# Scalar compares for ranks, and a lighter hand-shake in the second edge sweep of a graph kernel

## Chip, cores and metric

The kernel runs on one core of one Trainium2 chip. The metric is the device time of one execution in microseconds (us), the median of several runs.

## What is computed

Four graph layers run one after another over 6250 nodes with 128 features and 106250 edges that are sorted by receiver (`dst`). After each, the node rows are normalised: `x = layernorm(x + layer(x))`.

```python
msg = relu(concat([h[src], h[dst], w]) @ W1 + b1) @ W2 + b2     # layer 0
agg = segment_max(msg, dst); h = relu(concat([h, agg]) @ U1 + c1) @ U2 + c2
msg = relu(concat([v[src], factors[dst]]) @ Wm + bm)            # layer 1 (src: senders, dst: receivers)
agg = segment_sum(msg, src, 6250)                               # v + relu(concat([v, agg]) @ Wc + bc)
e = leaky_relu(e_l[src] + e_r[dst]); alpha = segment_softmax(e, dst)
out = segment_sum(alpha * Wh[src], dst)                         # layer 2, 4 heads of 32
h = relu(x @ W_in[0] + mean(x[src], dst) @ W_in[1])             # layer 3
h = h @ W_out[0] + mean(h[src], dst) @ W_out[1]
```

## The kernel before

The edges are cut into 208 blocks of 512 (`NB`, `EB`), each of four tiles of 128. Five sweeps go over all blocks: sweep 1 (layer 0, `edge_phase(1)`), sweep 2 (layer 1, `relation_phase`), sweep 3 (layer 2, `attention_phase`), sweeps 4 and 5 (layer 3, `edge_phase` again). A node phase follows each. Layer 1 sums over senders; its edges come in pairs that swap sender and receiver, plus loops, so this kernel walks them in receiver order too.

In every sweep a segmented scan on VectorE (DVE) runs along the edges: `scan = go * previous + value`, or a maximum. TensorE turns tiles of edges by features into features by edges ahead of the scan, and turns the scanned block back after it; ScalarE (ACT) copies it out of PSUM; it goes to memory as `scan_rows`. In sweeps 1, 3, 4 and 5 GpSimd (POOL) gathers the senders' rows with four indirect DMAs to a block (L1108, L1466). In sweep 2 the rows come ready from memory (`factor_rows`), and POOL gathers only for the following node phase (L739).

In sweeps 1, 2 and 3 the receivers' rows of a block are spread over its edges by a matrix product with a one-hot matrix `same`. DVE makes it: each of the 512 ranks of the block (type uint8, the same row on all partitions) is compared with a rank of the partition (`rank_cols`, float32), one column of `rank_cols` to each tile. It is one `tensor_tensor` of 128x512 to a block: L1261 in sweep 1, L1423 in sweep 2, L1639 in sweep 3. The scalar column is broadcast as the second tensor.

`steps(eng, n, unroll, (lag, f), ...)` writes the order of work of an engine: in step i each piece f is done for block i - lag, in the order of the list. In sweep 2:

```python
steps(sp, NB, SLOTS, (0, load), (7, store))
steps(pe, NB, SLOTS, (0, go_row), (0, senders), (2, turn_back))
steps(act, NB, SLOTS, (0, hidden), (2, keep_rows))
steps(v, NB, SLOTS, (0, same_receiver), (2, reduce))
```

SyncE (SP) issues all direct DMAs of sweep 2: four loads to a block (L1319 ranks, L1320 go marks, L1321 receiver rows, L1322 factor rows) into rings of four slots, and a store (L1328). It waits for `e_recv_free` (L1317), which ACT gives once TensorE has used a block's rows. TensorE's `go_row` (L1352) spreads the marks over 128 partitions in PSUM, `senders` (L1342, L1343) makes the layer's input, `turn_back` (L1362) turns the scanned block. Before each, it waits for data and for a buffer to be free. `chain` on ACT and DVE lets the engine wait for its own instruction before it gives its semaphores.

In sweep 3 the order on DVE is `(9, weigh), (10, add_up), (1, scores), (0, same_receiver), (1, stretch)`, on TensorE `(11, turn_back), (9, turn_weighted), (0, receiver_scores), (1, stretch)`. Every eighth step has a `stretch`: a softmax chain that goes back and forth between DVE, TensorE and ACT. The gathers go into 16 slots there, and into 8 in sweep 1.

Of the kernel before, what the change touches and what calls it, by code (L numbers as in the profile page):

```python
# [17 lines left out]
P = 128  # L18
# [5 lines left out]
EB = 512  # L24
CT = EB // P
NB = -(-E // EB)
# [59 lines left out]
def gnn_program(nc, a, out):  # L86
# [14 lines left out]
    with ctx:  # L101
# [128 lines left out]
        e_rows = sem("e_rows")  # L230
        stored = [sem(f"stored{s}") for s in range(SLOTS)]
        t_er_free = sem("t_er_free"); t_cb_free = sem("t_cb_free"); t_gath_free = sem("t_gath_free")
        e_rank = sem("e_rank"); e_rank_free = sem("e_rank_free")
        e_go = sem("e_go"); e_go_free = sem("e_go_free")
        over_cleared = sem("over_cleared"); over_made = sem("over_made")

        def part(q, s, unroll, n):
# [5 lines left out]
        with ExitStack() as pctx:  # L243
# [60 lines left out]
            with nc.Block() as block:  # L304
                @block.sync
                def _(sp):
# [78 lines left out]
                    sp.sem_inc(n_load, -32)  # L385

                    for free, n in ((n_agg_free, 2), (n_rows_free, 2), (n_x_bank_free, 1), (n_bank_free[7], 1), (n_bank_free[5], 1), (n_bank_free[3], 1),
                                    (e_gath_free, RING), (e_recv_free, SLOTS), (e_meta_free, SLOTS), (e_same_free, 2), (e_rank_free, 2), (e_go_free, 2),
                                    (e_pre_free, 2), (e_hid_free, 2), (e_msg_free, 2), (e_scan_free, 2), (e_back_free, 2),
                                    (t_er_free, 1), (t_cb_free, 1), (t_gath_free, 2 * STRETCH)):  # L390
                        sp.sem_inc(free, n)
# [694 lines left out]
        def edge_phase(k):  # L1086
# [157 lines left out]
            def vector(v):  # L1244
                if expands:
                    for s in range(2):
                        v.wait_ge(scattered[s], 16 * scatters * sum(GROUP_TILES[s::2]))
                    v.sem_inc(n_scat_all, 1)

                def chain(ins):  # L1250
                    ins.then_inc(v_done, 1)
                    v.wait_ge(v_done, 1)
                    v.sem_inc(v_done, -1)

                def same_receiver(q, s):

                    v.wait_ge(meta_in[s], 32)
                    v.sem_inc(meta_in[s], -32)
                    v.wait_ge(e_same_free, 1)
                    v.sem_inc(e_same_free, -1)  # L1260
                    v.tensor_tensor(same[s % 2][:, :, :], rank[s][:, :].rearrange("p (c e) -> p c e", e=P),  # L1261
                                    rank_cols[:, part(q, s, SLOTS, CT)].unsqueeze(2).to_broadcast([P, CT, P]), ALU.is_equal).then_inc(e_same, 1)

                def reduce(q, s):
                    if not expands:

                        v.wait_ge(meta_in[s], 16)
                        v.sem_inc(meta_in[s], -16)
                    v.wait_ge(e_msg if expands else e_pre, 1)
                    v.sem_inc(e_msg if expands else e_pre, -1)  # L1270
                    v.sem_inc(e_hid_free if expands else e_gath_free, 1)
                    v.wait_ge(e_scan_free, 1)
                    v.sem_inc(e_scan_free, -1)  # L1273
                    src = (msg_ps if expands else pre_ps)[s % 2][:, :]
                    go_on = meta[s][:, :]
                    chain(v.tensor_tensor_scan(scan[s % 2][:, :], go_on, src, scan[1 - s % 2][:, EB - 1:EB],  # L1276
                                               ALU.add if expands else ALU.mult, ALU.max if expands else ALU.add))
                    v.sem_inc(e_msg_free if expands else e_pre_free, 1)
                    v.sem_inc(e_meta_free, 1)
                    v.sem_inc(e_scan, 1)  # L1280

                if expands:
                    steps(v, NB, SLOTS, (0, same_receiver), (2, reduce))
                else:
                    steps(v, NB, SLOTS, (0, reduce))
# [3 lines left out]
        def relation_phase():  # L1289
# [42 lines left out]
            def tensor(pe):  # L1332
                def senders(q, s):

                    pe.wait_ge(e_same, 1)
                    pe.sem_inc(e_same, -1)
                    pe.wait_ge(e_pre_free, 1)
                    pe.sem_inc(e_pre_free, -1)
                    b = pre_ps[s % 2]
                    for c in range(CT):  # L1340
                        o = b[:, c * P:(c + 1) * P]
                        pe.matmul(o, factor[s][:, c, :], ident[:, :], start=True, stop=False, is_transpose=True)  # L1342
                        ins = pe.matmul(o, recv[s][:, c, :], same_ring[s][:, c, :], start=False, stop=True)  # L1343
                    ins.then_inc(e_pre, 1)

                def go_row(q, s):

                    pe.wait_ge(recv_in[s], 48)
                    pe.sem_inc(recv_in[s], -48)
                    pe.wait_ge(e_go_free, 1)  # L1350
                    pe.sem_inc(e_go_free, -1)
                    pe.matmul(go_ps[s % 2][:, :], ones_row[:, :], meta[s][0:1, :], start=True, stop=True).then_inc(e_go, 1)  # L1352

                def turn_back(q, s):

                    pe.wait_ge(e_scan, 1)
                    pe.sem_inc(e_scan, -1)

                    pe.wait_ge(e_back_free, 1)
                    pe.sem_inc(e_back_free, -1)  # L1360
                    for c in range(CT):
                        ins = pe.transpose(back_ps[s % 2][:, c * P:(c + 1) * P], scan[s % 2][:, c * P:(c + 1) * P], ident[:, :])  # L1362
                    ins.then_inc(e_back, 1)

                steps(pe, NB, SLOTS, (0, go_row), (0, senders), (2, turn_back))

            def scalar(act):
                def chain(ins):
# [4 lines left out]
                def hidden(q, s):  # L1373

                    act.wait_ge(e_pre, 1)
                    act.sem_inc(e_pre, -1)
                    act.sem_inc(e_recv_free, 1)
                    act.sem_inc(e_same_free, 1)
                    act.wait_ge(e_hid_free, 1)
                    act.sem_inc(e_hid_free, -1)  # L1380
                    chain(act.activation(hid[s % 2][:, :], pre_ps[s % 2][:, :], ACT.Relu, bias=bm[:, 0:1]))
                    act.sem_inc(e_pre_free, 1)
                    act.sem_inc(e_hid, 1)

                def keep_rows(q, s):

                    act.wait_ge(e_back, 1)
                    act.sem_inc(e_back, -1)
                    act.sem_inc(e_scan_free, 1)
                    if not (isinstance(q, int) and q == 0):  # L1390

                        act.wait_ge(stored[s], 16)
# [13 lines left out]
            def vector(v):  # L1406
                for s in range(2):
                    v.wait_ge(scattered[s], 16 * scatters * sum(GROUP_TILES[s::2]))
                v.sem_inc(n_scat_all, 1)
                v.sem_inc(e_same_free, 2)  # L1410

                def chain(ins):
                    ins.then_inc(v_done, 1)
                    v.wait_ge(v_done, 1)
                    v.sem_inc(v_done, -1)

                def same_receiver(q, s):

                    v.wait_ge(meta_in[s], 16)
                    v.sem_inc(meta_in[s], -16)  # L1420
                    v.wait_ge(e_same_free, 1)
                    v.sem_inc(e_same_free, -1)
                    v.tensor_tensor(same_ring[s][:, :, :], rank[s][:, :].rearrange("p (c e) -> p c e", e=P),  # L1423
                                    rank_cols[:, part(q, s, SLOTS, CT)].unsqueeze(2).to_broadcast([P, CT, P]), ALU.is_equal).then_inc(e_same, 1)

                def reduce(q, s):

                    v.wait_ge(e_go, 1)
                    v.sem_inc(e_go, -1)
                    v.wait_ge(e_hid, 1)  # L1430
                    v.sem_inc(e_hid, -1)
                    v.wait_ge(e_scan_free, 1)
                    v.sem_inc(e_scan_free, -1)  # L1433
                    chain(v.tensor_tensor_scan(scan[s % 2][:, :], go_ps[s % 2][:, :], hid[s % 2][:, :], scan[1 - s % 2][:, EB - 1:EB], ALU.mult, ALU.add))  # L1434
                    v.sem_inc(e_hid_free, 1)
                    v.sem_inc(e_go_free, 1)
                    v.sem_inc(e_scan, 1)

                steps(v, NB, SLOTS, (0, same_receiver), (2, reduce))

                v.wait_ge(e_same_free, 4)
                v.sem_inc(e_same_free, -2)
            return gpsimd, sync, tensor, scalar, vector

        def attention_phase():
# [176 lines left out]
            def vector(v):  # L1622
# [12 lines left out]
                def same_receiver(q, s):  # L1635

                    v.wait_ge(meta_in[s % SLOTS], 16)
                    v.sem_inc(meta_in[s % SLOTS], -16)
                    v.tensor_tensor(same[s % 2][:, :, :], rank[s % SLOTS][:, :].rearrange("p (c e) -> p c e", e=P),  # L1639
                                    rank_cols[:, part(q, s, U, CT)].unsqueeze(2).to_broadcast([P, CT, P]), ALU.is_equal).then_inc(e_same, 1)  # L1640

                def scores(q, s):

# [155 lines left out]
```

## Time and profile before

| what | us |
|---|---|
| median of 3 runs (5735.0 to 5740.53) | 5735.5 |
| the profiled execution: its own time | 5743.62 |
| the profiled execution: span of the trace | 5741.8 |
| busy in the span: TensorE / DVE / ACT / POOL | 3292.9 / 2408.0 / 1217.7 / 3673.6 |
| gathers of sweep 1, first start to last start | 357.5 to 1423.2 |
| rank compares of sweep 2, first start to last start | 1594.7 to 2167.5 |
| gathers of sweep 3, first start to last start | 2307.2 to 3382.6 |
| gathers of sweeps 4 and 5, first start to last start | 3503.2 to 5655.8 |

A span is the stretch from the first to the last instruction of the trace. "Idle before" is the time an engine stood still ahead of a group of instructions, and the name behind the arrow is what ended it; DVEq, ACTq, PEq, POOLq and SPq are the engines' own queues, where their semaphore instructions run.

### The profile page before, as it was taken

Reading aid. Unit: us, or ns where it says so; the run is one execution under the profiler, and the core shown is the slowest. Engines: PE = TensorE matmul, PEld = TensorE weight load, DVE = VectorE, ACT = ScalarE, POOL = GpSimd, SP = SyncE. Lnnn points to the kernel's source line nnn. Section 1 sums busy time; section 2 is a strip of 40 time slices with the busy share of each in tenths; the row PEclk is TensorE's granted clock in tenths of the full one; section 3 lists DMA queues with packets and bytes.
Section 4 is the critical chain, followed back from the end, with each engine's and each line's share of the span. In section 5 each row is a group of like instructions: output and inputs, shape, how many; then the busy total and the mean of one; then the engine's idle time right before and its main releaser. Section 6 shows DMA issues by size and latency. Waiting matters only on the chain. (4 is left out here: it accounts for less than half of the span.)

```text
span 5741.8 us, 88988 instructions
## 1 busy us (share of the span) xinstructions
PE 3292.9 (57%) x17957; PEld 2513.3 (44%) x17957; DVE 2408.0 (42%) x3908; ACT 1217.7 (21%) x2227; POOL 3673.6 (64%) x3810
## 2 busy tenths in 40 slices
PE   1268888888578886566666652333333443333335
PEld 0245555555356665456565652333333323333333
DVE  3323333333466665466666664222222222222224
ACT  0012222222234443122222221111111111111111
POOL 2277777777701004777777774777777767777776
PEclk7578999998799998678788875555555655555556
DMA  9969999998289996455555653444444444444443
GB/s 246 304 191 291 296 301 292 295 294 286 81 272 313 311 312 185 143 157 176 156 174 165 175 144 92 132 131 132 131 132 132 122 116 131 131 131 132 132 131 105
DMA packets 813159, 1087.16 MB, mean 189 GB/s; under 512 B 132097, under 2 KB 494202, under 8 KB 809690
## 3 DMA queue, kind: packets, MB, share of 16 engines
q1 hardware_dynamic: 371752, 390.56, 22.5%
q0 software_dynamic: 134688, 305.15, 21.1%
q10 hardware_dynamic: 306588, 390.09, 20.1%
q14 instruction: 96, 0.79, 0.0%
q8 instruction: 35, 0.57, 0.0%
HBM read 647.79 MB, written 437.96 MB: 189 GB/s over the span
## 5 line engine op out<-in xcount | busy, mean ns | idle before, releaser
L1108 POOL DMA_INDIRECT gath<-sender_table,src_cols x1664 | 1570.1, 944 | 576.3 <-issue 381.3
L1276 DVE TENSOR_TENSOR_SCAN scan<-meta,scan,bank 128x512 f32<-128x512 bf16 x624 | 798.6, 1280 | 1844.1 <-DVEq L1273 1833.9
L1163 PE MATMUL bank<-ident,gath 128*128 128x128 f32 x1664 | 464.0, 434 | 1276.1 <-DMA gath<-sender_table,src_cols 1276.1
L1466 POOL DMA_INDIRECT gath<-attention_table,src_cols x832 | 823.2, 989 | 262.9 <-issue 190.5
L1108 POOL DMA_INDIRECT gath<-joint_table,src_cols x832 | 813.3, 978 | 258.9 <-issue 188.7
L1163 PEld LDWEIGHTS bank<-ident,gath 128*128 128x128 f32 x1664 | 297.7, 217 | 1442.1 <-DMA gath<-sender_table,src_cols 1442.1
L1226 ACT ACTIVATE rows<-bank 128x512 f32<-128x512 f32 x624 | 372.6, 597 | 1995.4 <-ACTq L1224 1913.8
L1188 PE MATMUL bank<-ident,scan 128*128 128x128 f32 x2496 | 580.2, 379 | 4.8 <-PEq L1186 4.8
L1188 PEld LDWEIGHTS bank<-ident,scan 128*128 128x128 f32 x2496 | 478.9, 205 | 139.5 <-issue 139.5
L739 POOL DMA_INDIRECT gath<-scan_rows,end_i x147 | 140.9, 958 | 586.8 <-ACTq L1394 542.9
L1506 PE MATMUL bank<-recv,same 128*128 128x4 f32 x1664 | 225.5, 259 | 161.9 <-PEq L1504 161.6
L1261 DVE TENSOR_TENSOR same<-rank,rank_cols 128x512 f32<-128x512 uint8 x208 | 144.4, 694 | 412.7 <-DVEq L1260 391.1
L1506 PEld LDWEIGHTS bank<-recv,same 128*128 128x128 f32 x1664 | 218.1, 204 | 189.7 <-issue 189.7
L1170 PEld LDWEIGHTS bank<-same,recv 128*128 128x128 f32 x1664 | 224.4, 209 | 169.8 <-issue 169.8
L1211 ACT ACTIVATE hid<-bank,b 128x512 f32<-128x512 f32 x208 | 142.9, 687 | 698.9 <-ACTq L1210 653.7
L1730 DVE TENSOR_TENSOR_SCAN scan<-bank,scan,hid 128x512 f32<-128x512 f32 x208 | 266.6, 1282 | 55.2 <-DVEq L1729 49.3
L1170 PE MATMUL bank<-same,recv 128*128 128x128 f32 x1664 | 268.1, 310 | 0.0
L1434 DVE TENSOR_TENSOR_SCAN scan<-bank,scan,hid 128x512 f32<-128x512 f32 x208 | 265.5, 1277 | 3.5 <-DVEq L1433 2.9
L1178 PE MATMUL bank<-hid,w 128*128 128x512 f32 x416 | 249.8, 687 | 1.1 <-PEq L1177 1.1
L1168 PE MATMUL bank<-small,w1w 1*128 1x512 f32 x416 | 247.6, 676 | 0.0
L1554 PE MATMUL bank<-small,over_head 128*128 128x128 f32 x1664 | 244.9, 296 | 0.0
L1167 PE MATMUL bank<-ident,gath 128*128 128x128 f32 x832 | 139.5, 294 | 175.1 <-PEq L1158 154.7
(242 smaller groups left out, 5028.6 us busy)
## 6 DMA issues: line engine op xcount, KB each, us to landing
recv<-receiver_rows SPq DMA_DIRECT2D x624, 256.0 KB
scan_rows<-rows ACTq DMA_DIRECT2D x624, 256.0 KB
attention_scan_rows<-rows ACTq DMA_DIRECT2D x208, 264.0 KB
receiver_rows<-gath ACTq DMA_DIRECT2D x26, 2048.0 KB, 12.1
factor_rows<-gath ACTq DMA_DIRECT2D x208, 256.0 KB
gath<-factor_rows SPq DMA_DIRECT2D x208, 256.0 KB
scan_rows<-rows SPq DMA_DIRECT2D x208, 256.0 KB
meta<-edge_meta ACTq DMA_DIRECT2D x416, 128.0 KB
```

The costliest lines, as they stand in the source:

```text
L1108: pool.indirect_dma_start(out=landed[s][:, c, 0:width], out_offset=None, in_=table[:, :], in_offset=bass.IndirectOffsetOnAxis(ap=src_cols[ ...
L1163: ins = pe.transpose(b[:, c * P:(c + 1) * P], g[:, c, 0:F], ident[:, :])
L1168: pe.matmul(b[:, :], w1w[:, :], wrow[r][:, :], start=False, stop=False)
L1170: ins = pe.matmul(b[:, c * P:(c + 1) * P], recv[r][:, c, :], same[s % 2][:, c, :], start=False, stop=c == CT - 1)
L1178: pe.matmul(msg_ps[s % 2][:, :], w2[:, :], hid[s % 2][:, :], start=True, stop=True).then_inc(e_msg, 1)
L1188: ins = pe.transpose(back_ps[s % 2][:, c * P:(c + 1) * P], scan[s % 2][:, c * P:(c + 1) * P], ident[:, :])
L1226: chain(act.activation(rows_flat[r][:, :, :], back_ps[s % 2][:, :].rearrange("p (c f) -> p c f", f=F), ACT.Copy))
L1276: chain(v.tensor_tensor_scan(scan[s % 2][:, :], go_on, src, scan[1 - s % 2][:, EB - 1:EB], ALU.add if expands else ALU.mult, ALU.max if ex ...
L1434: chain(v.tensor_tensor_scan(scan[s % 2][:, :], go_ps[s % 2][:, :], hid[s % 2][:, :], scan[1 - s % 2][:, EB - 1:EB], ALU.mult, ALU.add))
L1466: pool.indirect_dma_start(out=gath[s][:, c, :], out_offset=None, in_=att_d[:, :], in_offset=bass.IndirectOffsetOnAxis(ap=src_cols[:, t:t + ...
L1506: ins = pe.matmul(er_ps[:, c * HEADS:(c + 1) * HEADS], same[s % 2][:, c, :], recv[s % SLOTS][:, c, 0:F:HID], start=True, stop=True)
L1730: chain(v.tensor_tensor_scan(scan[s % 2][:, :], fac_ps[s % 2][:, :], hid[s % 2][:, :], scan[1 - s % 2][:, EB - 1:EB], ALU.mult, ALU.add))
```

## The change

Sweep 2 (`relation_phase`):

- TensorE's order becomes `(2, turn_back), (0, go_row), (0, senders)`: in a step it turns block i - 2 back first, and then makes block i.
- `e_scan` is no longer counted down by TensorE but compared with the block's number, and taken back once at the end. DVE waits on it for its own preceding scan.
- Semaphores and waits go: on TensorE `e_pre_free` and `e_go_free`; on DVE `e_go`, `e_scan_free`, `e_same_free`, the chain behind the scan and two increments; on ACT `e_hid_free`, the chain behind `hidden`, and increments for `e_same_free`, `e_scan_free` and `e_pre_free`.

Sweeps 1 and 3: the one `tensor_tensor` of 128x512 becomes four `tensor_scalar` of 128x128, each with one column of `rank_cols` as its scalar; the last of them signals `e_same`. Sweep 2 keeps the `tensor_tensor`.

```diff
@@ edge_phase: same_receiver (sweep 1; sweep 3 alike)
-                    v.tensor_tensor(same[s % 2][:, :, :], rank[s][:, :].rearrange("p (c e) -> p c e", e=P),
-                                    rank_cols[:, part(q, s, SLOTS, CT)].unsqueeze(2).to_broadcast([P, CT, P]), ALU.is_equal).then_inc(e_same, 1)
+                    for c in range(CT):
+                        ins = v.tensor_scalar(same[s % 2][:, c, :], rank[s][:, c * P:(c + 1) * P], rank_cols[:, part(q, s * CT + c, SLOTS * CT, 1)], None, ALU.is_equal)
+                    ins.then_inc(e_same, 1)
@@ relation_phase: tensor
-                    pe.wait_ge(e_pre_free, 1)
-                    pe.sem_inc(e_pre_free, -1)
...
-                    pe.wait_ge(e_go_free, 1)
-                    pe.sem_inc(e_go_free, -1)
-                    pe.matmul(go_ps[s % 2][:, :], ones_row[:, :], meta[s][0:1, :], start=True, stop=True).then_inc(e_go, 1)
+                    pe.matmul(go_ps[s % 2][:, :], ones_row[:, :], meta[s][0:1, :], start=True, stop=True)
...
-                    pe.wait_ge(e_scan, 1)
-                    pe.sem_inc(e_scan, -1)
+                    pe.wait_ge(e_scan, q * SLOTS + (s + 1))
...
-                steps(pe, NB, SLOTS, (0, go_row), (0, senders), (2, turn_back))
+                steps(pe, NB, SLOTS, (2, turn_back), (0, go_row), (0, senders))
+                pe.sem_inc(e_scan, -NB)
@@ relation_phase: scalar
-                    act.sem_inc(e_same_free, 1)
-                    act.wait_ge(e_hid_free, 1)
-                    act.sem_inc(e_hid_free, -1)
-                    chain(act.activation(hid[s % 2][:, :], pre_ps[s % 2][:, :], ACT.Relu, bias=bm[:, 0:1]))
-                    act.sem_inc(e_pre_free, 1)
-                    act.sem_inc(e_hid, 1)
+                    act.activation(hid[s % 2][:, :], pre_ps[s % 2][:, :], ACT.Relu, bias=bm[:, 0:1]).then_inc(e_hid, 1)
...
-                    act.sem_inc(e_scan_free, 1)
@@ relation_phase: vector
-                    v.wait_ge(e_same_free, 1)
-                    v.sem_inc(e_same_free, -1)
...
-                    v.wait_ge(e_go, 1)
-                    v.sem_inc(e_go, -1)
                     v.wait_ge(e_hid, 1)
                     v.sem_inc(e_hid, -1)
-                    v.wait_ge(e_scan_free, 1)
-                    v.sem_inc(e_scan_free, -1)
-                    chain(v.tensor_tensor_scan(scan[s % 2][:, :], go_ps[s % 2][:, :], hid[s % 2][:, :], scan[1 - s % 2][:, EB - 1:EB], ALU.mult, ALU.add))
-                    v.sem_inc(e_hid_free, 1)
-                    v.sem_inc(e_go_free, 1)
-                    v.sem_inc(e_scan, 1)
+                    if not (isinstance(q, int) and q * SLOTS + s == 0):
+                        v.wait_ge(e_scan, q * SLOTS + s)
+                    v.tensor_tensor_scan(scan[s % 2][:, :], go_ps[s % 2][:, :], hid[s % 2][:, :], scan[1 - s % 2][:, EB - 1:EB], ALU.mult, ALU.add).then_inc(e_scan, 1)
```

## Rows read from the trace of the kernel before

**Rows 1.** Busy time by stretch: gathers of sweep 1, sweep 2, gathers of sweep 3.

```profile
358.00:1424.00 1066.00, 916.42 (x4106) 551.58 (x4106) 401.29 (x410) 261.55 (x408) 812.74 (x832) 0.90 0.92 292
1591.00:2178.00 587.00, 480.60 (x3540) 386.14 (x3540) 394.22 (x418) 267.14 (x416) 34.71 (x34) 0.99 0.94 306
2307.00:3384.00 1077.00, 698.43 (x5107) 645.08 (x5107) 682.30 (x1362) 277.18 (x668) 823.26 (x833) 0.81 0.57 165
```

**Rows 2.** SP's own waits, whole span: total us, times, longest.

```profile
SPq L1318 <- SPq L1318: 7.8, 10, 1.6
```

**Rows 3.** Timeline of SP in sweep 2: rank loads four blocks apart.

```profile
1701.85 0.33 SPq L1319 DMA_DIRECT2D rank<-edge_rank  x1
...
1712.91 0.33 SPq L1319 DMA_DIRECT2D rank<-edge_rank  x1
```

**Rows 4.** Timeline of DVE in sweep 2: the compares of two blocks in turn.

```profile
1803.76 0.69 DVE L1423 TENSOR_TENSOR same<-rank,rank_cols 128x512 f32<-128x512 uint8 x1 [1.07 <-DVEq L1422]
...
1806.38 0.69 DVE L1423 TENSOR_TENSOR same<-rank,rank_cols 128x512 f32<-128x512 uint8 x1 [0.74 <-DVEq L1420]
```

**Rows 5.** Gathers of sweep 1, and of sweeps 4 and 5: min/median/max ns.

```profile
L1108 POOL DMA_INDIRECT gath<-joint_table,src_cols x832: 942/946/1470, 357.5 to 1423.2; - x167
...
L1108 POOL DMA_INDIRECT gath<-sender_table,src_cols x1664: 938/944/962, 3503.2 to 5655.8; - x185
```

**Rows 6.** Groups of gathers, sweeps 3 and 1: busy us, mean ns, idle before.

```profile
L1466 POOL DMA_INDIRECT gath<-attention_table,src_cols x832 | 823.2, 989 | 262.9 <-issue 190.5 <-POOLq L1463 67.2 <-ACTq L1595 4.6
L1108 POOL DMA_INDIRECT gath<-joint_table,src_cols x832 | 813.3, 978 | 258.9 <-issue 188.7 <-POOLq L1105 53.6 <-POOLq L1101 14.1
```

**Rows 7.** Timeline in sweep 1: a compare and the gather that starts under it.

```profile
800.95 0.69 DVE L1261 TENSOR_TENSOR same<-rank,rank_cols 128x512 f32<-128x512 uint8 x1 [1.07 <-DVEq L1260]
801.14 1.33 POOL L1108 DMA_INDIRECT gath<-joint_table,src_cols  x1 [0.30 <-issue]
```

**Rows 8.** Timeline in the last node phase: four scalar instructions and gathers.

```profile
5705.51 1.12 DVE L895 TENSOR_SCALAR x_nm<-recv,mv,rstd 128x128 f32<-128x128 f32 x4 [0.15 <-DVEq L814]
...
5705.95 0.97 POOL L739 DMA_INDIRECT gath<-scan_rows,end_i  x1 [0.30 <-issue]
```

**Rows 9.** Groups of DVE instructions: busy us, mean ns; L515 stands in the preparation.

```profile
L1261 DVE TENSOR_TENSOR same<-rank,rank_cols 128x512 f32<-128x512 uint8 x208 | 144.4, 694 | 412.7 <-DVEq L1260 391.1 <-ACTq L1205 12.6 <-DVEq L1258 7.1
...
L895 DVE TENSOR_SCALAR x_nm<-recv,mv,rstd 128x128 f32<-128x128 f32 x196 | 55.2, 352 | 8.2 <-DVEq L814 7.8 <-DVE rstd L893 0.2
...
L515 DVE TENSOR_SCALAR x_nm<-gath 128x896 f32<-128x896 f32 x1 | 0.6, 627 | 0.1
```

**Rows 10.** Timeline of DVE in a stretch of sweep 3: two scalar instructions.

```profile
3355.75 0.24 DVE L1694 TENSOR_SCALAR spread<-tile_of,small 128x32 f32<-128x32 f32 x1
3355.90 0.23 DVE L1695 TENSOR_SCALAR spread<-tile_of,small 128x32 f32<-128x32 f32 x1
```

**Rows 11.** Waits of TensorE in sweep 1 (400 to 1400 us): total, times, longest.

```profile
PE bank L1167 <- DMA gath<-joint_table,src_cols: 15.3, 9, 3.0
```

**Rows 12.** Timeline of sweep 3: one way around DVE, TensorE and ACT.

```profile
3336.10 0.69 DVE L1639 TENSOR_TENSOR same<-rank,rank_cols 128x512 f32<-128x512 uint8 x1
...
3336.93 1.03 PE L1506 MATMUL bank<-recv,same 128*128 128x4 f32 x8 [0.88 <-PEq L1504]
...
3340.25 0.60 ACT L1596 ACTIVATE hid<-bank 128x512 f32<-128x512 f32 x1 [0.81 <-ACTq L1594]
...
3341.11 1.28 DVE L1730 TENSOR_TENSOR_SCAN scan<-bank,scan,hid 128x512 f32<-128x512 f32 x1 [0.47 <-ACTq L1597]
...
3343.08 0.69 DVE L1639 TENSOR_TENSOR same<-rank,rank_cols 128x512 f32<-128x512 uint8 x1
```

**Rows 13.** Timeline of DVE: the first scan of two stretches of sweep 3.

```profile
3307.66 0.42 DVE L1666 TENSOR_TENSOR_SCAN small<-bar_c,bank 128x128 f32<-128x128 f32 x1 [1.43 <-DVEq L1663]
...
3348.62 0.42 DVE L1666 TENSOR_TENSOR_SCAN small<-bar_c,bank 128x128 f32<-128x128 f32 x1 [1.40 <-DVEq L1663]
```

**Rows 14.** Sweep 3 (2400 to 3400 us): idle time ended by a gather's landing.

```profile
  DMA gath<-attention_table,src_cols: 10.0, 6
```

More of the change, by code:

```diff
@@ L232, in gnn_program @@
         t_er_free = sem("t_er_free"); t_cb_free = sem("t_cb_free"); t_gath_free = sem("t_gath_free")
-        e_rank = sem("e_rank"); e_rank_free = sem("e_rank_free")
-        e_go = sem("e_go"); e_go_free = sem("e_go_free")
         over_cleared = sem("over_cleared"); over_made = sem("over_made")
@@ L387, in _ @@
                     for free, n in ((n_agg_free, 2), (n_rows_free, 2), (n_x_bank_free, 1), (n_bank_free[7], 1), (n_bank_free[5], 1), (n_bank_free[3], 1),
-                                    (e_gath_free, RING), (e_recv_free, SLOTS), (e_meta_free, SLOTS), (e_same_free, 2), (e_rank_free, 2), (e_go_free, 2),
+                                    (e_gath_free, RING), (e_recv_free, SLOTS), (e_meta_free, SLOTS), (e_same_free, 2),
                                     (e_pre_free, 2), (e_hid_free, 2), (e_msg_free, 2), (e_scan_free, 2), (e_back_free, 2),
@@ L1409, in vector @@
                 v.sem_inc(n_scat_all, 1)
[L1410 to L1415, printed above, removed]
                 def same_receiver(q, s):
@@ L1426, in reduce @@
                 def reduce(q, s):
-                    v.wait_ge(e_go, 1)
-                    v.sem_inc(e_go, -1)
                     v.wait_ge(e_hid, 1)
                     v.sem_inc(e_hid, -1)
-                    v.wait_ge(e_scan_free, 1)
-                    v.sem_inc(e_scan_free, -1)
-                    chain(v.tensor_tensor_scan(scan[s % 2][:, :], go_ps[s % 2][:, :], hid[s % 2][:, :], scan[1 - s % 2][:, EB - 1:EB], ALU.mult, ALU.add))
-                    v.sem_inc(e_hid_free, 1)
-                    v.sem_inc(e_go_free, 1)
-                    v.sem_inc(e_scan, 1)
+                    if not (isinstance(q, int) and q * SLOTS + s == 0):
+                        v.wait_ge(e_scan, q * SLOTS + s)
+                    v.tensor_tensor_scan(scan[s % 2][:, :], go_ps[s % 2][:, :], hid[s % 2][:, :], scan[1 - s % 2][:, EB - 1:EB], ALU.mult, ALU.add).then_inc(e_scan, 1)
                 steps(v, NB, SLOTS, (0, same_receiver), (2, reduce))
-                v.wait_ge(e_same_free, 4)
-                v.sem_inc(e_same_free, -2)
             return gpsimd, sync, tensor, scalar, vector
@@ L1638, in same_receiver @@
                     v.sem_inc(meta_in[s % SLOTS], -16)
-                    v.tensor_tensor(same[s % 2][:, :, :], rank[s % SLOTS][:, :].rearrange("p (c e) -> p c e", e=P),
-                                    rank_cols[:, part(q, s, U, CT)].unsqueeze(2).to_broadcast([P, CT, P]), ALU.is_equal).then_inc(e_same, 1)
+                    for c in range(CT):
+                        ins = v.tensor_scalar(same[s % 2][:, c, :], rank[s % SLOTS][:, c * P:(c + 1) * P], rank_cols[:, part(q, s * CT + c, U * CT, 1)], None, ALU.is_equal)
+                    ins.then_inc(e_same, 1)
                 def scores(q, s):
```

## The prediction

> **What bounds the kernel now.** I read the busy time by stretch first, since the five sweeps have different limits [rows 1]. The change touches three of them; sweeps 4 and 5 and the node phases stay as they are.
>
> Sweep 2 moves 306 GB/s with the DMA engines 94% busy, while TensorE has 82% and DVE 67% of the 587 us [rows 1]. Then I asked who sets that pace. SP's own waits name it: over all 208 blocks SP stood at L1318, where it waits for a free slot, for 7.8 us [rows 2]. So SP is nearly always issuing, and its loads come at its own pace: from one rank load to the one four blocks later, 11.06 us [rows 3], 2.765 us a block, and 208 of them are 575 of the sweep's 587 us. DVE is close behind: where its compare waits for nothing but its own queue, one step is 1806.38 - 1803.76 = 2.62 us [rows 4]. What the reader is to see: the waits that the change takes from sweep 2 are on engines that are faster than SP.
>
> Sweeps 1 and 3 look bound by POOL: one gather follows on another, with 0.3 us between them and hardly a wait for a slot [rows 6]. But their length is not constant. In sweeps 4 and 5 no gather is over 962 ns; in sweep 1 the median is as low, and the longest takes 1470 [rows 5]. A gather that starts under a rank compare is a long one: the compare runs 800.95 to 801.64, the gather starts at 801.14 and takes 1.33 us instead of 0.95 [rows 7]. The surplus over 944 ns is (978 - 944) x 832 = 28 us in sweep 1 and (989 - 944) x 832 = 37 us in sweep 3 [rows 6], 27 in sweep 1 against its own median of 946 ns [rows 5]. In sweep 3 there are two such `tensor_tensor` to a block, the compare and `weigh`, so I give the compare half of it, 19 us.
>
> **Sweep 2, part by part.** SP's order, its instructions and DMAs are the same, so its 2.765 us a block stay. DVE loses seven queue instructions, the wait for its own scan ahead of them among these, and gets one: the 0.74 us that it stood idle ahead of a compare [rows 4] can shrink to nearly nothing, 2.62 to about 2 us. TensorE's reorder puts `turn_back` (four turns) between a scan and the next `senders`. What is late then is the block that needs the scan two blocks back; That way around, for two blocks, holds TensorE's work for one block (480.6 / 208 = 2.31 us), ACT's copy (267.1 / 416 = 0.64), the scan (394.2 / 208 - 0.61 = 1.28, where 0.61 is the part of the compare ahead of it) [rows 1] and three changes of engine at 0.14 us, the distance from a compare's end to TensorE's answer in rows 12: 4.65 us, and I allow up to 5.2 for semaphores. That is 2.3 to 2.6 us a block, still below SP's 2.765. What is queued behind TensorE's wait for `e_scan` is `go_row` and `senders`; ACT's `hidden` waits for them, and with it the slot that SP wants. Gain: at most the 7.8 us of SP's waits, plus a shorter tail behind the last load; I take half of the waits and 2 us of tail, **-6**. The bounds are -17 (all waits and 9 us of tail) and +10, if the reorder makes SP wait 0.05 us a block.
>
> **The price of the new compare.** No row has a uint8 source with a scalar column. L895 is nearest: 128x128 with two scalar columns, four in 1.12 us, so one each (1.12 - 0.35) / 3 = 0.26 us [rows 8, 9]. With one scalar column and 32 elements the distance is 0.15 us [rows 10]. L515 does 896 elements in 627 ns, 0.70 ns each with everything in it [rows 9], so more than one element a cycle, where the compare has 694 / 512 = 1.36; the 96 elements between 32 and 128 cost about 0.05 us at that rate. I take 0.20 us as distance, and the run of four as 3 x 0.20 + 0.29 = 0.89 us, against 0.69 now: **+0.2 us** a block. Bounds: +0.35 with L895's distance, +0.5 if a uint8 source goes at one element a cycle (0.28 apart, the last 0.35).
>
> **What the new compare does to a gather.** Rows 8 have the four scalar instructions beside a gather: the one that starts at 5705.95, under them, takes 0.97 us. That is 0.03 over a plain one, where a `tensor_tensor` costs 0.38. So I count 0.02 us for each block, 4 us a sweep. The Trainium skill (SBUF — State Buffer, "SBUF: two separate sides") explains both: a two-input DVE instruction holds the read port that GpSimd shares, and a `tensor_scalar` in a two-port mode locks the whole pair, so that GpSimd "cannot write the descriptors". By that rule the new form could block a gather wholly; this trace shows 0.03 us for it [rows 8]. What it would give is a rival below.
>
> **Sweep 1.** POOL can gain 27 - 4 = 23 us. But TensorE waited for a landing gather only 15.3 us, 9 times, in 1000 us of the sweep [rows 11]; the rest of its idle time ends by other things (ranks, receiver rows and marks from a DMA that is 92% busy [rows 1]). POOL's gathers would then run ahead into the ring of eight, and the blocks behind them would gain the 15.3 us at most. Against it stands the compare's +0.2 us in the way around four load slots, +0.05 a block if it is always critical, +10; I take +4. **-11**, bounds -23 and +10.
>
> **Sweep 3.** POOL needs 1.294 us a gather, (3382.6 - 2307.2) / 831, or 41.4 us for a stretch of eight blocks. DVE's cycle from stretch to stretch is 3348.62 - 3307.66 = 40.96 us [rows 13]: the two are nearly tied, and over 1000 us DVE waited for gathers only 10.0 us [rows 14]. Here the compare stands on the path. It starts at 3336.10, TensorE's `receiver_scores` waits for its end and starts at 3336.93, `turn_back` and `turn_weighted` stand behind it in TensorE's queue, ACT's copy follows at 3340.25, the scan of it at 3341.11, and the compare two blocks on at 3343.08 [rows 12]: 6.98 us for two blocks. 0.2 us more there is 0.1 a block over seven blocks, and 0.2 once in the stretch, where DVE works alone: 0.9 us a stretch, 24 stretches, +22. Off goes the 10 us of waiting for gathers: **+12**. POOL falls to about 40.8 us a stretch (41.4 less 19 / 26), below DVE's 41.9, so its gain buys nothing more. Bounds: -15 (POOL's 19 - 4 comes through in full and the way round gives way) and +27 (0.35 us a block: 1.5 us a stretch, 37 less 10); +43 at one element a cycle.
>
> **Sum.** -6 - 11 + 12 = -5 us, from 5743.6 us of the profiled execution to 5738.6. It lies 8 us above the median, so on the median's scale 5735.5 - 5 = 5730.5.
>
> **Rivals.**
> 1. *The gathers' surplus comes back in full.* If POOL really sets the pace of sweeps 1 and 3, they give -23 and -15; with sweep 2's -6 that is -44: 5691. For it: POOL never waits [rows 6]. Against: TensorE in sweep 1 hardly waits for gathers [rows 11], and DVE's cycle in sweep 3 is as long as POOL's [rows 13]. 20%.
> 2. *Sweep 1 in full, sweep 3 as forecast.* -23 + 12 - 6 = -17: 5718. It needs the DMA to carry 2% more than 292 GB/s in sweep 1; sweep 2 has 306 [rows 1]. 20%.
> 3. *DVE bounds sweep 3 (slower).* The new compare takes 0.35 us more, not 0.2, on the way of rows 12: +27 in sweep 3, 0 in sweep 1 and -2 in sweep 2, +25: 5760; at one element a cycle 5776. It decides from about 0.3 us a block on, against the 10 us that DVE has to spare. For it: L895's 0.26 us apart [rows 8]. 18%.
> 4. *The scalar form blocks gathers (slower).* A run of 0.89 us in every 1.27 us between gathers' starts meets 0.7 of them and holds one for half its length: 0.31 us x 208 = 65 us a sweep in place of 27 and 19, so +84 on POOL's side: about 5810. It is the page's rule at full strength, and rows 8 speak against it. 5%.
> 5. *Forecast*, with these off-setting: 37%.
>
> **How the numbers follow.** I take 0.2% (11 us) as what a measurement of this kernel can tell from no change. The forecast's own range is 5715 to 5748. Rivals 1 and 2 are faster, 3 and 4 slower; the forecast's tails go to both sides about evenly, mostly same. Faster 0.42, same 0.35, slower 0.23. The range that holds 8 in 10 leaves out half of rival 1 and the far part of 3 and 4: 5694 to 5763. Predicted: 5730.
>
> **What would show each step.** The gathers of sweep 1 should have a mean of at most 950 ns and none over 1.1 us; if they don't, the port argument is wrong. The last gather of sweep 1 should start some 23 us earlier, the last scan only about 11. In sweep 2 SP's rank loads stay 11.06 us apart over four blocks; DVE's idle time ahead of compares is cut, and the sweep is 6 us shorter. The four compares should lie 0.20 us apart. In sweep 3 the cycle from stretch to stretch goes from 41.0 to 41.9 us, with TensorE's L1506 still right behind the compare. The prediction fails if the scalar form takes over 0.3 us apiece, if sweep 1's end follows the gathers, or if SP begins to wait at L1318.

## The result, and the profile after

The changed kernel takes 5831.1 us (median of 4 runs, 5814.9 to 5837.3); the kernel before took 5738.0 in the same set. The ratio is 1.0158, 95% interval 1.0134 to 1.0181: 93 us slower. The forecast was 5730 with a range to 5763. The profiled execution of after took 5814.86 us, with a span of 5813.1, 71 us over the span before; it is the fastest of the four.

Busy time of the changed kernel by stretch, for the same three stretches as [rows 1]. The columns, there too: the stretch and its length; busy us (and instructions) of TensorE, of its weight loads, DVE, ACT and POOL; TensorE's granted clock as a share of full speed; the busy share of the DMA engines; GB/s.

```profile
359.00:1408.00 1049.00, 901.13 (x4032) 545.04 (x4032) 439.57 (x1013) 257.29 (x401) 787.92 (x832) 0.90 0.92 293
1591.00:2172.00 581.00, 502.68 (x3540) 389.99 (x3540) 395.03 (x418) 252.84 (x416) 33.57 (x34) 0.99 0.94 309
2299.00:3429.00 1130.00, 705.87 (x4953) 647.54 (x4954) 705.33 (x1939) 268.91 (x648) 805.64 (x832) 0.77 0.54 155
```

The last line holds the loss: the gathers of sweep 3 now take 1130 us where they took 1077, though each is shorter. The groups of gathers, first by busy time and mean, then by shortest, median and longest, answer to [rows 6] and [rows 5]:

```profile
L1440 POOL DMA_INDIRECT gath<-attention_table,src_cols x832 | 805.7, 968 | 333.2 <-issue 221.3 <-POOLq L1437 109.4 <-ACTq L1569 2.4
L1106 POOL DMA_INDIRECT gath<-joint_table,src_cols x832 | 788.6, 948 | 265.8 <-issue 205.3 <-POOLq L1103 32.9 <-POOLq L1099 25.4
```

```profile
L1106 POOL DMA_INDIRECT gath<-joint_table,src_cols x832: 940/946/1038, 359.9 to 1407.7; - x167
```

In sweep 1 the mean is 948 ns and the longest 1038: the argument on gathers held. The last gather starts 15.5 us earlier, but the last scan only 2.5 us earlier (1437.3 for 1439.8).

The scans of sweeps 2 and 3, first to last start, in the changed kernel:

```profile
L1414 DVE TENSOR_TENSOR_SCAN scan<-bank,scan,hid x208: 1270/1278/1284, 1597.8 to 2167.1; 128x512 f32<-128x512 f32 x104
L1705 DVE TENSOR_TENSOR_SCAN scan<-bank,scan,hid x208: 1269/1282/1286, 2361.6 to 3491.2; 128x512 f32<-128x512 f32 x104
```

and in the kernel before:

```profile
L1434 DVE TENSOR_TENSOR_SCAN scan<-bank,scan,hid x208: 1275/1276/1284, 1600.8 to 2173.1; 128x512 f32<-128x512 f32 x104
L1730 DVE TENSOR_TENSOR_SCAN scan<-bank,scan,hid x208: 1275/1282/1285, 2368.9 to 3421.6; 128x512 f32<-128x512 f32 x104
```

Sweep 2 is 569.3 us for 572.3, sweep 3 is 1129.6 for 1052.7: +77 us, more than the whole difference of the two spans. The first scans of three stretches of sweep 3 in the changed kernel (they answer to [rows 13]):

```profile
3011.07 0.42 DVE L1641 TENSOR_TENSOR_SCAN small<-bar_c,bank 128x128 f32<-128x128 f32 x1 [1.54 <-DVEq L1638]
3053.08 0.42 DVE L1641 TENSOR_TENSOR_SCAN small<-bar_c,bank 128x128 f32<-128x128 f32 x1 [1.40 <-DVEq L1638]
3100.07 0.42 DVE L1641 TENSOR_TENSOR_SCAN small<-bar_c,bank 128x128 f32<-128x128 f32 x1 [1.43 <-DVEq L1638]
```

One stretch is 42.01 us, the next 46.99. The loop of sweep 3 is unrolled over 16 blocks, so every second stretch crosses its branch. Over the whole loop the ten stretches with a branch take 46.3 to 48.7 us, and the ten without one 42.0 to 43.7, mean 42.8, where 41.9 was forecast. DVE's timeline there:

```profile
2730.33 0.88 DVE L1614 TENSOR_SCALAR same<-rank,rank_cols 128x128 f32<-128x128 uint8 x4
2736.53 0.69 DVE L1696 TENSOR_TENSOR gath<-gath,small 128x512 f32<-128x512 f32 x1 [5.32 <-issue]
```

The four compares take 0.88 us, as forecast. Then DVE stands still for 5.32 us, ended by nothing that a semaphore shows. In its queue the loop's compare-and-branch (L68) starts at 2730.8 us and the next instruction at 2736.4; at each of the ten branches of this loop the kernel before needs 0.3 us for the same step. In the changed kernel:

```profile
L68 DVEq COMPARE_BRANCH  x1: 63/63/63, 2730.8 to 2730.8; - x1
L68 DVEq MOVE  x1: 36/36/36, 2736.4 to 2736.4; - x1
```

DVE's waits at that place, 2400 to 3400 us (total, times, longest), which the kernel before does not have at its `weigh`:

```profile
DVE gath L1696 <- issue: 47.4, 10, 5.4
```

Instructions are transferred meanwhile. The packets of instruction queue q14 from 2600 to 3400 us, before and after (packets, MB, share of 16 engines):

```profile
q14 instruction: 8, 0.07, 0.0%
```

```profile
q14 instruction: 49, 0.40, 0.1%
```

Each of these packets is of 8192 bytes, 128 instructions of 64 bytes. In the whole span there are 96 before and 148 after; 41 of the 52 more fall in these 800 us, which brings them to five or six a turn of the loop. A second instruction queue, q8, has packets of 16384 bytes, 35 before and 34 after. The views don't name the engine that a packet is for; that the ones more on q14 are DVE's is read from where they fall: one starts inside each of DVE's ten waits.

### The profile page after: what moved, and what is told of

Same layout as the page of the kernel before. It is cut to its first block and busy times, and to the rows that moved or that the text cites. A ratio compares the mean times of both kernels' runs of the same rounds, so it can differ in the third digit from the quotient of the medians.

```text
span 5813.1 us, 88433 instructions
## 1 busy us (share of the span) xinstructions
PE 3336.3 (57%) x17957; PEld 2536.9 (44%) x17957; DVE 2497.4 (43%) x5156; ACT 1203.7 (21%) x2227; POOL 3634.1 (63%) x3810
## 5 line engine op out<-in xcount | busy, mean ns | idle before, releaser
L1161 PE MATMUL bank<-ident,gath 128*128 128x128 f32 x1664 | 464.0, 434 | 1276.9 <-DMA gath<-sender_table,src_cols 1276.9
L1440 POOL DMA_INDIRECT gath<-attention_table,src_cols x832 | 805.7, 968 | 333.2 <-issue 221.3
L1106 POOL DMA_INDIRECT gath<-joint_table,src_cols x832 | 788.6, 948 | 265.8 <-issue 205.3
L1260 DVE TENSOR_SCALAR same<-rank,rank_cols 128x128 f32<-128x128 uint8 x832 | 191.2, 304 | 394.2 <-DVEq L1258 365.7
L1339 PE MATMUL bank<-ident,gath 128*128 128x128 f32 x832 | 238.9, 287 | 0.0
```

Of the source, the lines that this page charges most:

```text
L1106: pool.indirect_dma_start(out=landed[s][:, c, 0:width], out_offset=None, in_=table[:, :], in_offset=bass.IndirectOffsetOnAxis(ap=src_cols[ ...
L1161: ins = pe.transpose(b[:, c * P:(c + 1) * P], g[:, c, 0:F], ident[:, :])
L1440: pool.indirect_dma_start(out=gath[s][:, c, :], out_offset=None, in_=att_d[:, :], in_offset=bass.IndirectOffsetOnAxis(ap=src_cols[:, t:t + ...
```

## The experiments

"Before" is the kernel before on the same chip in the same set. Two of the five sets fell on chips where the kernel before takes 7315 and 7387 us: there POOL waits for slots in every sweep (552.8 us in sweep 3 in `e1_sweep2_only`, where the kernel before has 67.2 on the first chip), and small effects on DVE can hide behind that.

**1. Each part alone.** `e1_sweep2_only`: the changed kernel with the one `tensor_tensor` back in sweeps 1 and 3. `e2_sweep1_only` and `e3_sweep3_only`: the kernel before with this edit in one sweep.

```diff
-v.tensor_tensor(same..., ALU.is_equal).then_inc(e_same, 1)
+for c in range(CT):
+    ins = v.tensor_scalar(same[s % 2][:, c, :], rank..., rank_cols[...one column...], None, ALU.is_equal)
+ins.then_inc(e_same, 1)
```

> The change of sweep 2 alone; sweeps 1 and 3 keep the one tensor_tensor. The trace of the changed kernel has sweep 2 about 3.5 us shorter. Theory A (the loss sits in sweep 3, where VectorE's longer loop waits at its branch for instructions): -2 to -6 us against before, and VectorE's cycle from stretch to stretch in sweep 3 stays 41.0 us. Rival B (the reorder of sweep 2 leaves the later sweeps in a worse phase, or something of it costs there): a good part of the +93 us stands here too, above +20.

> The kernel before with the four scalar compares in sweep 1 alone. Its VectorE loop goes from 51 to 75 instructions a turn. Theory A: no wait for instructions at that size, and sweep 1 limited by what the loads bring: the mean gather falls from 978 to about 948 ns, but the end of the sweep moves by only -2 to -4 us. Rival B (each scalar compare is dear wherever it stands): slower by 10 us or more, since the rank compare takes 0.2 us more in 208 blocks.

> The kernel before with the four scalar compares in sweep 3 alone. Both theories expect most of the loss here, +75 to +100 us. They differ in where: theory A has VectorE stand still once in every turn of its loop (16 blocks) for about 5 us between the last queue instruction of a turn and the first of the next, 12 times, and the other stretches 42.0 us long; rival B (the compare holds TensorE or GpSimd up) has every stretch of eight blocks longer by the same 3 us.

`e4_pads_only` keeps all compares and makes the loop of sweep 3 longer:

```diff
 def add_up(q, s):
-    chain(v.tensor_tensor_scan(scan...))
+    v.tensor_tensor_scan(scan...).then_inc(v_done, 1)
+    for j in range(3):
+        v.sem_inc(pad, 1)
+        v.sem_inc(pad, -1)
+    v.wait_ge(v_done, 1)
+    v.sem_inc(v_done, -1)
```

> The kernel before, tensor_tensor kept everywhere. In sweep 3 six semaphore increments to a block are added to VectorE's queue behind the scan, on a semaphore that nobody reads, so that its loop has 403 instructions a turn in place of 307, as many as the changed kernel; they are written where VectorE waits for its scan anyway. Theory A: +45 to +70 us, from a wait of 4 to 5 us once a turn of 16 blocks, and packets of the instruction queue in sweep 3 in number as in the changed kernel (about 38 in 600 us, where the kernel before has 5). Rival B (the scalar compares themselves are what is dear): between -2 and +8 us, no such wait.

Measured, with 7314.8 us before: 1.0000 (0.9980 to 1.0020) for sweep 2 alone, 1.0028 (1.0012 to 1.0045) for sweep 1, 0.9977 (0.9958 to 0.9995) for sweep 3, 1.0032 (1.0018 to 1.0046) for the padding. The times decide little here, since sweep 3 takes 1536 to 1572 us in all four; sweep 1's part costs 24 us. The traces do: `e3` and `e4` both have 10 waits of some 4 us at the branch and 147 and 148 instruction packets, the other two have no such wait and 96. So the waits come without any scalar compare. Whether they cost time had to be seen on a chip like the first.

**2. The same on a chip with 5737.6 us before.** `e3` and `e4` again, and two new ones. In `e6` the scalar compares of sweep 3 take their column from a small copy, which leaves 342 instructions in the loop:

```diff
+if s == 0:
+    chain(v.tensor_copy(cols_now[:, :], rank_cols[:, part(q, 0, 1, U * CT)]))
 for c in range(CT):
-    ins = v.tensor_scalar(..., rank_cols[:, part(q, s * CT + c, U * CT, 1)], None, ALU.is_equal)
+    ins = v.tensor_scalar(..., cols_now[:, s * CT + c:s * CT + c + 1], None, ALU.is_equal)
```

`e7` is the changed kernel with the `tensor_tensor` back in sweep 3 alone.

> The scalar compares in sweep 3 alone, once more, on another chip if one is given: on the first chip the kernel before took 7315 us in place of 5736, its gathers landed late there, and a wait of VectorE in sweep 3 could hide behind them. Theory A (wait for instructions at VectorE's loop branch): where the kernel before takes about 5736 us, +75 to +95 us, with the wait of 4 to 5 us once in 16 blocks as on the first chip (10 waits, 41.7 us); where it takes 7315 us again, no more than 15 us either way. Rival B (what the first chip showed, no loss, is the rule and the +93 us come from elsewhere): within 15 us of before on every chip.

> The padded VectorE loop (403 instructions a turn, tensor_tensor kept), once more beside the run above. Theory A: +45 to +75 us where the kernel before takes 5736 us, from the waits at the branch (10 waits of 4.2 us on the first chip); on a chip where gathers land late +10 to +30. Rival B (scalar compares hold other engines up, the wait at the branch is harmless): below +10 us.

> The kernel before with scalar compares in sweep 3, but once in a turn of 16 blocks the 64 rank columns are copied to a small tile, and the compares take their column from there, at an address fixed at build time. That saves the register instructions: about 341 instructions in VectorE's loop in place of 403. Theory A, with the limit between 341 and 403: no wait at the branch, packets of the instruction queue as in the kernel before (96 in the whole run), the stretch 42.0 us long, +10 to +25 us where the kernel before takes 5736 us. If the limit lies between 307 and 341: waits as with 403, +60 to +90. Rival B: +60 to +90 without waits at the branch.

> The changed kernel with sweep 3's compare back to the one tensor_tensor: sweep 2's part and sweep 1's scalar compares stay. By the changed kernel's trace sweep 2 gives -3.5 us and sweep 1 -2.6 us: -4 to -9 us against before under theory A, with 96 packets of the instruction queue. If something outside sweep 3 has a share in the loss: +5 us or more.

| run | us | ratio (95%) | DVE loop, instructions | instruction packets |
|---|---|---|---|---|
| `e3_sweep3_again` | 5812.3 | 1.0131 (1.0114 to 1.0148) | 403 | 147 |
| `e4_pads_again` | 5804.3 | 1.0121 (1.0104 to 1.0138) | 403 | 148 |
| `e6_columns_copied` | 5804.6 | 1.0119 (1.0102 to 1.0136) | 342 | 147 |
| `e7_without_sweep3` | 5811.3 | 1.0119 (1.0098 to 1.0140) | 307 | 146 |

The padding alone costs 67 us, so rival B, in which the waits are harmless, is out. But theory A as I had it, with the loop's length as the cause, falls with `e7`: its loop in sweep 3 is the unchanged one of 307 instructions, and it waits at the branch as well (10 times, 40.0 us). What differs is where the loop lies. Sweeps 1 and 2 stand ahead of it in DVE's stream, and their edits had moved it.

**3. Only the place of the loop.** Counted in the built program, DVE's loop of sweep 3 starts at instruction 2125 in the kernel before and at 2091 in `e7`. Theory C: a loop that touches three blocks of 128 instructions stays, one that touches four is fetched anew each turn. `g1` is the kernel before, with this ahead of sweep 3 on DVE and nothing else; `g2` is `e7` with 40 of them, `g3` is `e6` with 38.

```diff
 def vector(v):    # sweep 3
+    for j in range(94 // 2):
+        v.sem_inc(pad, 1)
+        v.sem_inc(pad, -1)
```

> The kernel before, with 94 semaphore increments that nobody reads put ahead of sweep 3 on VectorE, where it waits some 10 us for its first ranks. Nothing inside any loop is changed: sweep 3's loop has its 307 instructions, only 94 further on in VectorE's stream (the built program has it start at instruction 2219 in place of 2125). Theory C, formed after the runs without sweep 3's scalar compares were slow too (307 instructions at 2091, waits at the branch of 4.2 to 4.7 us): the stream comes in blocks of 128 instructions (the 8192-byte packets of the instruction queue), a loop that touches three of them stays, one that touches four is fetched anew at each turn. 2219 lies in its block as 2091 does: +60 to +75 us, 10 or 11 waits at the branch, about 147 packets. Theory A as it was (the number of instructions in the loop decides) and rival B: within 5 us of before, 96 packets.

> The changed kernel with one tensor_tensor in sweep 3 (the run that was 74 us slower), and 40 such increments ahead of sweep 3 on VectorE: its loop of 307 instructions starts at 2131 in place of 2091. By theory C, from the kernels with this loop so far (without waits at 2125, 2043 and 2173, places 77, 123 and 125 in a block of 128; with waits at 2091, place 43), place 83 lies among those without waits: 4 to 9 us faster than before, 96 packets. If theory C is wrong and something in sweeps 1 and 2 makes sweep 3 slow: +65 to +75 as without the shift.

> The run with scalar compares in sweep 3 that take their columns from a copied tile (342 instructions in the loop, start 2225, waits at the branch, +67 us), with 38 increments ahead of sweep 3: start 2263. Theory C: 342 instructions can touch three blocks only if they start in the first 42 places; with the start of the blocks as the other runs bound it, 2263 does so and 2225 does not. No waits at the branch, 96 packets; what is left is the price of the scalar compares themselves in sweep 3, for which the prediction had +12 (bounds -15 and +43): +5 to +25 us. Without theory C: +60 to +75.

> Sweep 2's part of the change alone, once more: on the first chip (7315 us for the kernel before) it made no difference, 1.000 with 0.998 to 1.002. Its loop of sweep 3 starts at 2043 and had no waits at the branch there. Theory C: -2 to -6 us where the kernel before takes 5736 us, 96 packets. If sweep 2's reorder costs something later: +5 us or more.

| run | us (before 5751.9) | ratio (95%) | packets | sweep 3, first to last scan |
|---|---|---|---|---|
| `g1_shift_only` | 5814.8 | 1.0112 (1.0091 to 1.0133) | 147 | 1113.1 |
| `g2_no_sweep3_shifted` | 5770.2 | 1.0031 (1.0017 to 1.0046) | 96 | 1058.7 |
| `g3_columns_shifted` | 5779.2 | 1.0043 (1.0031 to 1.0056) | 97 | 1079.7 |
| `e1_sweep2_again` | 5752.4 | 1.0005 (0.9991 to 1.0019) | 95 | 1055.6 |

`g1` has not one instruction changed inside a loop and is 63 us slower. DVE's timeline at a branch of it, and its waits there:

```profile
2737.06 0.69 DVE L1643 TENSOR_TENSOR same<-rank,rank_cols 128x512 f32<-128x512 uint8 x1
2741.77 0.69 DVE L1725 TENSOR_TENSOR gath<-gath,small 128x512 f32<-128x512 f32 x1 [4.01 <-issue]
```

```profile
DVE gath L1725 <- issue: 41.2, 10, 4.8
```

In each of these ten waits a packet of q14 starts 2.6 to 3.5 us after the branch does, and DVE goes on some 1.8 us after the packet's start.

In `g2` and `g3` the waits are gone with a shift of 40 and 38 instructions: sweep 3 goes from 1113.1 us (`e7`) to 1058.7, and from 1112.9 (`e6`) to 1079.7. Packets and waits agree with theory C in all kernels, with one position of the blocks:

| waits | loops by length: start (its place in a block of 128) |
|---|---|
| no | 307: 2125 (77), 2043 (123), 2173 (125), 2149 (101), 2131 (83); 342: 2263 (87) |
| yes | 307: 2091 (43), 2219 (43); 342: 2225 (49); 403: 2187 (11), 2221 (45), 2257 (81) |

A block's start has to lie between places 50 and 77 of this count for all of them; the count leaves out what a loader puts ahead, so only differences mean something. A loop of 403 touches at least four blocks wherever it starts. That the blocks are of 128 is inferred from the packets' size and from this fit, which has one free number; three of the twelve places were forecast before they ran (`g1`, `g2`, `g3`). Blocks of 256 don't fit: a loop of 307 would touch a third one only from the last 50 places of a block, and 2091 and 2219, 128 apart, cannot both lie there.

`g2` came out 18 us slower, where 4 to 9 faster was expected, and `e1` without a difference. That leaves sweep 1.

**4. Sweep 1.** From first to last scan it takes 1052.7, 1051.8 and 1050.2 us with the `tensor_tensor` on the second set's chip and 1058.7 with the scalar compares (`e7`); on the third's 1057.1, 1061.4 and 1058.6 against 1066.5 (`g2`). Each is one profiled execution. `h1` is the kernel of `e2`, scalar compares in sweep 1 alone. `h2` delays the signal of the `tensor_tensor` and leaves all else:

```diff
-    ..., ALU.is_equal).then_inc(e_same, 1)
+    ..., ALU.is_equal).then_inc(v_done, 1)
+v.wait_ge(v_done, 1)
+v.sem_inc(v_done, -1)
+v.sem_inc(e_same, 1)
```

> Scalar compares in sweep 1 alone, on another chip than the first. Sweep 3's loop starts at 2173, where it had no waits on the first chip. From first to last scan, sweep 1 took 1052.7, 1051.8 and 1050.2 us with tensor_tensor and 1058.7 with the scalar compares on one chip, 1057.1, 1061.4 and 1058.6 against 1066.5 on another, so each theory has to give +7 us here in place of the -11 that was predicted. Theory D (the compare's signal comes 0.2 us later on the way around the four load slots): +5 to +9 us. Theory E (the seven us are a phase of the transfers or chance): -3 to +3.

> The kernel before, tensor_tensor kept everywhere, but in sweep 1 the compare's signal goes out by way of a wait and a separate increment on VectorE, so some 0.2 us later, as late as the last of four scalar compares. Gathers are disturbed by the tensor_tensor as before. Theory D: +5 to +9 us, like the scalar compares. Theory F (the gathers that the scalar compares let run ahead crowd the loads of ranks and receivers' rows on the same 16 DMA engines, which are 93% busy): -2 to +3 us here, and the whole loss only with the scalar compares.

> Scalar compares in sweep 1 alone, a third time: the first two chips took 7315 and 7387 us for the kernel before (their gathers land late) and gave +24 and +49 us. If this chip takes about 5736 us: theory F (the gathers that run ahead crowd the loads) and theory D (the later signal) both +5 to +9 us; chance, -3 to +3.

> The later signal with tensor_tensor kept, again beside the scalar compares: on the chip of 7387 us it gave +8 us (ratio 1.0011, 0.9993 to 1.0028) where the scalar compares gave +49. Theory F: -2 to +3 us here where the scalar compares cost 5 to 9; theory D: both alike.

With 7386.9 us before: `h1` 1.0068 (1.0043 to 1.0093), 49 us, `h2` 1.0011 (0.9993 to 1.0028). With 5747.1 us before: `h1` 5762.2, 1.0023 (1.0011 to 1.0035), `h2` 5750.3, 1.0007 (0.9998 to 1.0016). The gathers of sweep 1 in `h1` and in `h2` on the last chip:

```profile
L1108 POOL DMA_INDIRECT gath<-joint_table,src_cols x832 | 789.2, 949 | 279.3 <-issue 210.4 <-POOLq L1105 36.8 <-POOLq L1101 28.2
```

```profile
L1108 POOL DMA_INDIRECT gath<-joint_table,src_cols x832 | 813.9, 978 | 258.8 <-issue 192.9 <-POOLq L1101 35.8 <-POOLq L1105 23.8
```

The scalar compares do shorten the gathers by 29 ns each, and the kernel is 15 us slower with them. The later signal costs 3 us, too little to tell from nothing, so theory D is at most a small part; and `h1`'s loss is clear of noise on both chips, outside theory E's -3 to +3. What the traces add: from a block's last gather to its scan pass 25.1 us in `h2` and 35.0 in `h1` (mean of blocks 20 to 199; 20.2 in the kernel before and 29.6 in the changed one), so POOL's gain goes into running two blocks further ahead, on DMA engines that are 92% busy in both. That the earlier gathers crowd the loads (theory F) fits, but was only argued; a gather held back on purpose beside scalar compares was not tried. Nor do the traces place the 15 us in sweep 1. The two profiled executions are 34.7 us apart (`h1`'s, 5779.4 us, is 17 above its median, `h2`'s 6 below): 4.7 us of it lie in sweep 1 (1070.5 against 1065.8), 18.7 in sweep 3 (1061.9 against 1043.2) and 10.2 ahead of the first scan, both with the same code. Why scalar compares in sweep 1 cost 15 us, and where, stays open.

On the chips of 5736 to 5752 us no version beat the kernel before: sweep 2's part alone is level with it. On the chip of 7315 us `e3` was 0.2% faster, its interval just clear of 1.

## Why the prediction was wrong

**The step that failed** is sweep 3's sum, +12 us, where the profiled pair shows +77. It priced the compare by the way around DVE, TensorE and ACT and let the rest of a stretch stand, so the time in which DVE waits for its own code stood at nothing. It never asked what the added and removed instructions do to DVE's loop as code, and no rival did. The compare's four instructions and their three further register instructions bring the loop from 307 to 403, over three blocks; DVE then waits 4 to 5.5 us at each of the ten branches back, 39 to 50 us in all in the runs on the faster chips, and the waits and what queues behind them cost 67 us with the padding alone (`e4`), 63 with the shift alone (`g1`). The edits of sweeps 1 and 2 would have been enough: they moved the unchanged loop to 2091.

**Scalar compares in sweep 3** by themselves: `g3`, with the waits gone, is 27 us slower than before (1.0043). Its sweep 3 is 24 us longer than `e1`'s on the same chip. The prediction had +22 for the way around less 10 for gathers, so +12. The 10 us of waiting for gathers did go (12.6 us in `e1`, none in `g3`, 2400 to 3400 us), and the sweep is longer by 24 all the same: the deduction is not to be seen in the time. Whether it bought nothing, or the way around costs more than 22, the runs don't tell apart; `g3` also copies the columns once a turn. The compare's own time was right (0.88 us for 0.89), the stretch was not: mean 42.8 us without a branch, for 41.9. Rival 3's time in sweep 3, +27, is near this, but by another mechanism, so that is luck: the compare did not take the 0.35 us more that it supposed.

**Sweep 1**: forecast -11. From first to last scan the profiled pair shows -2.3, pairs on one chip +5 to +9, and `h1` is +15 for the whole kernel. The first half held (gathers of 948 ns; the surplus was the `tensor_tensor`'s); the second did not: the gain of gathers that land ahead of need was counted as 11 when it was nothing or less. The 15.3 us of [rows 11] were no stock to draw on: in the changed kernel TensorE's waits for gathers fall to 5.5 us and the sweep gains 2.3; in `h1` none is left and `h2`, with the `tensor_tensor`, has only 3.5.

**Sweep 2**: forecast -6. The profiled pair shows -3.0, and the runs of the part alone, +0.5 us (0.9991 to 1.0019), cannot tell it from nothing. SP's rank loads four blocks apart are 10.99 us (11.06 in [rows 3]) and its waits for a slot 5.4 us (7.8 in [rows 2]). DVE's idle time ahead of its compares hardly falls, from 180 to 170 us (1600 to 2160 us), though it has fewer waits to pass: SP's loads set the pace, as forecast.

```profile
1700.31 0.33 SPq L1318 DMA_DIRECT2D rank<-edge_rank  x1
...
1711.30 0.33 SPq L1318 DMA_DIRECT2D rank<-edge_rank  x1
```

```profile
SPq L1317 <- SPq L1317: 5.4, 6, 1.8
```

**Rivals.** 1 and 2, the gathers' surplus in full, are out: gathers got short and nothing came of it. 4, blocked gathers, is out by 948 ns: the lock that the prediction names for the scalar form does not show, so it explains nothing in rows 8. The single parts, +75 (`e3`) + 15 (`h1`) + 0.5 (`e1`), make 90 of the 93 us, though from three chips, and they need not add: `e7`, the other two parts together, is +74 by the place of the loop alone. One working of the prediction is off and changed nothing: 96 elements at 0.70 ns are 0.07 us, not 0.05.

## What to carry to other kernels

Before counting cycles of an edit, count instructions: how many the loop it stands in gets, and how far it moves the loops behind it on the same engine. An idle stretch just behind a loop's branch that ends with "issue", once a turn, and more packets on the instruction queue are the sign; a few dozen idle instructions ahead of the loop, put where the engine waits anyway, tell in one run whether the loop's place is the cause. And a producer that is ahead already may gain nothing from being faster, whatever its busy share.

## What was unexpected of the hardware

DVE loops of 307 instructions, 19.6 KB, ran without a wait at five places and waited 4 to 5 us a turn at two others, with 146 and 147 packets of 8192 bytes in place of 96; one of 342 did either, by its place. The Trainium skill (Runtime: NRT & Kernel Launch, "Instruction fetch mechanics") says that a taken branch to code outside the window that the engine holds forces a fetch before it goes on; the trace agrees (5.32 us at such a branch). The page has that window as two pages of 16 KiB, 512 instructions; here q14's packets are of 8 KB (q8's of 16), loops of 307 were fetched anew, and the runs fit three blocks of 128 and not blocks of 256, so the measurement decides.

The kernel before takes 5736 to 5752 us on four chips and 7315 and 7387 on two others, with the same instructions. Sweeps 4 and 5, whose code no run changed, take 1264 to 1294 us each from first to last scan in the runs on these two, for 1036. The expectations say that gathers land late there; the traces say something else. In sweeps 4 and 5 TensorE starts on a block 0.4 us (median) after the last packet of its gathers in the kernel before and 28 us after it in `e1_sweep2_only`, while those packets end as early after POOL's instruction (1.3 us for 1.5). What TensorE waits for stays open. And sweep 3 with unchanged code varied from 1043 to 1062 us between runs on the faster chips, with gathers of 976 to 1000 ns; that its DVE and POOL cycles are nearly tied may be why, and was not tested.
